# The expert layer of a fused conv, attention and mixture kernel: its two halves interleaved, pooling on column tiles, scatter by image pairs

## What is computed

```python
t = t + attn(ln(t)); t = t + ffn(ln(t))        # t: (16, 3136, 32); _L1_ffn_ref:
logits = einsum('bsd,ed->bse', x, gate_w) + gate_b          # 16 experts
probs = softmax(logits, axis=1)                              # over the positions
topv, topi = top_k(probs, 8)                                 # 8 positions per image and expert
pooled = einsum('bked,bke->bed', x[topi], topv)              # weighted sum of the 8 tokens
h = gelu([pooled, 1] @ weight1[e])                           # 33 -> 128
out = [h, 1] @ weight2[e]                                    # 129 -> 32
outputs[b, topi] += topv * out                               # scattered back
```

## Time and profile before

| | us |
|---|---|
| median of 3 runs (lowest, highest) | 3361.59 (3358.89, 3364.82) |
| the profiled execution's own time | 3363.74 |
| its span, first to last instruction | 3361.9 |
| mean granted TensorE clock, share of full | 0.951 |
| last attention instruction on PE ends | 3157.3 |
| first half of the expert layer starts on PE | 3169.96 |
| second half starts on PE | 3252.42 |
| last addition ends, stores start | 3334.5 |

### The profile page before, as it was taken

How to read it: one execution, slowest core, us unless ns; L and a number is a source line. 1 busy time by engine, 2 the same in 40 slices (tenths; PEclk the granted TensorE clock), 3 DMA queues, 4 the chain that set the end, 5 groups by cost and what they waited for, 6 DMA issues and landing times.

```text
span 3361.9 us, 66302 instructions
## 1 busy us (share of the span) xinstructions
PE 2950.1 (88%) x23401; PEld 1258.3 (37%) x23401; DVE 2471.9 (74%) x3210; ACT 2200.9 (65%) x3825; POOL 619.9 (18%) x497
## 2 busy tenths in 40 slices
PE   3788888888868999999999999999999999999775
PEld 2444444444435233333333333333333333333354
DVE  6788888888847877767777767777777777787342
ACT  2477776676755577767767767767777776777520
POOL 0444444444430101101101101001001011011100
PEclk7899999999989899999999999999999999999876
DMA  3000000000018010110110110101101101100022
GB/s 83 6 15 14 14 14 14 14 14 14 14 56 303 7 20 1 20 21 1 20 21 1 21 20 2 21 3 19 20 2 20 20 2 21 20 1 1 7 37 40
DMA packets 130451, 81.57 MB, mean 24 GB/s; under 512 B 111285, under 2 KB 120086, under 8 KB 129174
## 3 DMA queue, kind: packets, MB, share of 16 engines
q1 hardware_dynamic: 128629, 78.26, 9.5%
q10 hardware_dynamic: 1568, 0.04, 0.0%
HBM read 39.57 MB, written 32.11 MB: 21 GB/s over the span
## 4 chain that ended last, share of the span: by engine, by line
PE 59%; DVE 14%; issue 12%; POOL 6%; ACT 6%; DMA 2%; ACTq 1%; POOLq 0%; SPq 0%; DVEq 0%
PE ps L1531 18%; PE ps L1508 15%; PE ps L1478 14%; DVE arena L1117 7%; POOL arena L512 3%; PE ps L1541 2%; POOL arena L518 2%; ACT arena L667 1%; ACT L693 1%; PE ps L1358 1%; PE ps L1590 1%; PE ps L1490 1%; DMA arena<-in_x 1%; DVE arena L964 1%; POOL arena L528 1%
## 5 line engine op out<-in xcount | busy, mean ns | idle before, releaser
L1117 DVE TENSOR_REDUCE arena<-ps 128x2 f32<-128x896 f32 (+1 forms) x1408 | 1485.1, 1082 | 460.6 <-PE ps L1478 447.1
L800 ACT ACTIVATE arena<-ps 128x512 f32<-128x512 f32 (+1 forms) x2464 | 1377.4, 595 | 553.8 <-PE ps L1508 543.4
L1508 PE MATMUL ps<-arena 97*128 97x512 f16 (+1 forms) x2800 | 898.9, 360 | 24.6 <-issue 20.0
L1478 PE MATMUL ps<-arena 96*128 96x448 f16 x2800 | 775.9, 360 | 36.0 <-DVE arena L1117 27.1
L1531 PE MATMUL ps<-arena 128*32 128x512 f32 (+1 forms) x6176 | 685.4, 521 | 17.5 <-DVE arena L1139 17.0
L1508 PEld LDWEIGHTS ps<-arena 97*128 97x128 f16 (+1 forms) x2800 | 255.7, 100 | 708.0 <-ACT arena L800 462.5
L1478 PEld LDWEIGHTS ps<-arena 96*128 96x128 f16 x2800 | 256.8, 99 | 322.7 <-DVE arena L1117 108.3
L577 POOL TENSOR_TENSOR tok<-arena,tok 128x128 f32 (+3 forms) x112 | 47.9, 427 | 1585.4 <-DVE arena L1139 1585.4
L518 POOL TENSOR_TENSOR arena<-arena 113x784 f32<-113x784 f32 x128 | 192.4, 1503 | 428.9 <-DVE arena L967 428.9
L1531 PEld LDWEIGHTS ps<-arena 128*32 128x32 f32 x6176 | 131.5, 111 | 255.0 <-ACT arena L800 138.7
L512 POOL TENSOR_TENSOR arena<-arena 113x784 f32<-113x784 f32 x128 | 192.2, 1502 | 128.6 <-DVE arena L958 128.6
(11 more groups left out here) (180 smaller groups left out, 2787.5 us busy)
## 6 DMA issues: line engine op xcount, KB each, us to landing
arena<-qk_scratch SPq DMA_DIRECT2D x96, 196.0 KB, 4.1
qk_scratch<-arena SPq DMA_DIRECT2D x16, 448.0 KB, 4.9
arena<-ximg SPq DMA_DIRECT2D x16, 400.0 KB, 7.0
arena<-in_x SPq DMA_DIRECT2D x4, 1568.0 KB, 8.5
xa_scratch<-arena SPq DMA_DIRECT2D x32, 196.0 KB, 1.9
res_scratch<-arena SPq DMA_DIRECT2D x32, 196.0 KB, 2.1
arena<-xa_scratch SPq DMA_DIRECT2D x4, 1568.0 KB, 8.0
arena<-res_scratch SPq DMA_DIRECT2D x4, 1568.0 KB, 11.9
```

What stands on the lines that cost most here:

```text
L800: act.activation(pk[0:rows, x % DEPTH, QC * m:QC * m + n], ps[0:rows, w % SB, 0:n], ACT.Exp, scale=float(C) ** -0.5).then_inc(att["exp"], 1)
L1117: dve.tensor_reduce(mxp[0:rows, p, 2 * u:2 * u + k], ps[0:rows, at_:at_ + k, 0:KN], AX_X, ALU.max)\
L1478: last = pe.matmul(ps[0:rows, MB + 2 * (j % 2) + n % 2, 0:KN], q2[p][0:96, T * t:T * t + rows], k2[p][0:96, KN * m:KN * m + KN], start=Tru ...
L1508: last = pe.matmul(ps[0:rows, bank, at_ % QC:at_ % QC + chunk_cols(c)], k2[p][0:97, T * t:T * t + rows], q2[p][0:97, QC * c:QC * c + chunk ...
```

## The change

1. The halves are taken in the order `HALVES = (1, 0)`: first slots 8 to 15, which do not hold the last image. Only the second half's token columns wait for `att["xf"]`.
2. The last image's difference, square and product move from POOL to DVE, between its copies; the power stays on POOL.
3. Token columns and logits go chunk by chunk (up to 512 positions), with both groups of a chunk side by side: logits of a chunk are two matmuls, 64 output partitions each, and one ACT copy of all 128. In the first half ACT copies group 0 and DVE group 1, in the second ACT both. `token_exp(0)` stands on ACT ahead of chunk 1 of the second half, `token_scale(0)` ahead of chunk 5.
4. Selection: `not_equal` goes; ACT scales the exponentials by the reciprocal in two parts, DVE makes one product for each.
5. `mt` is copied by ACT alone. Pooling is one matmul for each image and tile (200 a half), 32 output partitions (a column tile) and 16 columns; 4 ACT copies take the result.
6. The bias of the second expert matrix is added by DVE in the copy to `eo` (`w2b` as 32 x 16), so the 16 one-row matmuls go.
7. Scatter goes by image pair: for each pair `r` and tile one matmul over 32 rows of `mk` with 64 columns, up to 8 tiles in a bank, and 4 DVE additions a pair. 200 matmuls a half.
8. PE's order interleaves the second half's pooling and experts with the first half's scatter.
9. Stores wait for one pair (4 additions) and issue its two images. The expert weights are loaded before attention's loop; ACT and DVE wait for the stores of `qk_scratch` before image 0, since buffers moved onto their source.

```diff
+        HALVES = (1, 0)
-            sp.wait_ge(att["xf"], B + 1)
-            for h in range(B // PB):
-                sp.wait_ge(moe["add"], NT * (h + 1))
+            for o in range(2):
+                for r in range(PB // 2):
+                    sp.wait_ge(moe["add"], 16 * o + 4 * r + 4)
...
+            act.wait_ge(prep["stored_a"], 64 * G)
+            act.wait_ge(prep["stored_b"], 64 * G)
...
@@ ACT @@
+            for n in range(NX):
+                token_columns(0, n, 0)
+                if n:
+                    logits_copy(0, n - 1)
+            logits_copy(0, NX - 1)
+            for n in range(NX):
+                if n == 1:
+                    token_exp(0)
+                if n == 5:
+                    token_scale(0)
+                token_columns(1, n, 0)
+                token_columns(1, n, 1)
+                if n:
+                    logits_copy(1, n - 1)
+            logits_copy(1, NX - 1)
+            weights_copy(0)
+            token_exp(1)
+            token_scale(1)
+            pooled_copy(0)
+            expert_gelu(0)
+            weights_copy(1)
+            pooled_copy(1)
+            expert_gelu(1)
...
@@ DVE @@
+            token_columns(0)
+            dve.memset(pooled[C:C + 1, :, :], 1.0).then_inc(moe["ones"], 1)
+            token_columns(1)
             sum_slot(B)
             mean_slot(B)
+            token_columns(2)
+            center_last()
+            token_columns(3)
+            square_last()
+            token_columns(4)
             square_sum(B)
             variance_slot(B)
+            token_columns(5)
+            token_columns(6)
+            normalize_last()
+            top_tokens(0)
+            top_tokens(1)
+            expert_out(0)
+            for r in range(4):
+                add_pair(0, r)
+            expert_out(1)
+            for r in range(4):
+                add_pair(1, r)
...
-                        last = pe.matmul(ps[:, 7, 64 * gg:64 * gg + 64], xf[0:rows, t, GB * g:GB * g + GB, :].rearrange("p b c -> p (b c)"),
-                                         mt[0:rows, t, 64 * gg:64 * gg + 64], start=(t == 0), stop=(t == NT - 1))
+                        for j in range(GB):
+                            b = GB * gg + j
+                            last = pe.matmul(ps[C * j:C * j + C, 7, E * gg:E * gg + E], xf[0:rows, t, half_slot(o, b), :],
+                                             mt[0:rows, t, E * b:E * b + E], start=(t == 0), stop=(t == NT - 1),
...
-                    pe.matmul(ps[0:rows, 3 + t % 4, 0:PB * C], mk[:, T * t:T * t + rows], bdo[:, :], start=True, stop=True)\
+                        last = pe.matmul(ps[0:rows, tg, 2 * C * (t % 8):2 * C * (t % 8 + 1)],
+                                         mk[o][C * r:C * r + C, T * t:T * t + rows],
+                                         bdo[C * r:C * r + C, :, :].rearrange("p b c -> p (b c)"), start=True, stop=True)
...
@@ PE @@
+            for o in range(2):
+                if o:
+                    pe.wait_ge(att["xf"], B + 1)
+                for n in range(NX):
+                    token_columns(o, n)
+                    if n:
+                        logits(o, n - 1)
+                logits(o, NX - 1)
+            weight_rows(0)
+            pool_tokens(0)
+            expert_hidden(0)
+            expert_out(0)
+            out_rows(0)
+            weight_rows(1)
+            scatter_pair(0, 0)
+            pool_tokens(1)
+            scatter_pair(0, 1)
+            expert_hidden(1)
+            scatter_pair(0, 2)
+            expert_out(1)
+            scatter_pair(0, 3)
+            out_rows(1)
+            for r in range(4):
+                scatter_pair(1, r)
```

More of the change, by code:

```diff
@@ L820, in _ @@
                         sums_copy(B - 1, c)
[L823 to L841, removed]
@@ new lines, in expert_gelu @@
+            def expert_gelu(o):
+                act.wait_ge(moe["hid"], o + 1)
+                if o:
+                    act.wait_ge(moe["out"], 1)
+                act.activation(eh[:, :], ps[:, 4, 0:E * PB], ACT.Gelu).then_inc(moe["gelu"], 1)
+            for n in range(NX):
[12 more added lines that the diff above has]
+                    logits_copy(1, n - 1)
@@ L1207, in _ @@
[L1207 to L1242, removed]
-                    dve.wait_ge(moe["scat"], NT * h + t + 1)
-                    v = tok[0:rows, PB * h:PB * (h + 1), t, :]
-                    dve.tensor_tensor(v, v, ps[0:rows, 3 + t % 4, 0:PB * C].rearrange("p (b c) -> p b c", b=PB), ALU.add)\
-                       .then_inc(moe["add"], 1)
@@ new lines, in token_columns, with logits @@
+                    last.then_inc(moe["xft"], 1)
+            def logits(o, n):
+                f = o * NX + n
+                for gg in range(2):
+                    pe.wait_ge(moe[f"xftc{gg}"], f + 1)
+                if f >= 3:
+                    pe.wait_ge(moe["logitc"], f - 2)
+                for gg in range(2):
+                    last = pe.matmul(ps[64 * gg:64 * gg + 64, f % 3, 0:chunk_cols(n)],
+                                     wgate[:, :, :].rearrange("p j e -> p (j e)"), xft[:, f % 3, gg, 0:chunk_cols(n)],
+                                     start=True, stop=True)
+                last.then_inc(moe["logit"], 1)
@@ new lines, in weight_rows @@
+            def weight_rows(o):
+                pe.wait_ge(moe["mk"], 2 * o + 2)
+                for n in range(NX):
+                    if o == 0 and n == 0:
+                        pe.wait_ge(moe["logitc"], 2 * NX)
+                    if NX * o + n >= 4:
+                        pe.wait_ge(moe["mtc"], NX * o + n - 3 if n >= 4 else NX * o)
+                    for t in chunk_tiles(n):
+                        rows = tile_rows(t)
+                        last = pe.transpose(ps[0:rows, n % 4, 128 * (t % 4):128 * (t % 4) + 128],
+                                            mk[o][:, T * t:T * t + rows], ident(128))
@@ L1669, in _, with expert_hidden @@
+                last.then_inc(moe["pool"], 1)
+            def expert_hidden(o):
+                pe.wait_ge(moe["poolc"], o + 1)
+                if o:
+                    pe.wait_ge(moe["gelu"], 1)
+                else:
+                    pe.wait_ge(moe["weights"], 48)
+                    pe.wait_ge(moe["ones"], 1)
                 for e in range(E):
-                    last = pe.matmul(ps[:, 0, PB * e:PB * (e + 1)], w1e[:, e, :], pooled[:, e, :], start=True, stop=True)
+                    last = pe.matmul(ps[:, 4, PB * e:PB * (e + 1)], w1e[:, e, :], pooled[:, e, :], start=True, stop=True)
@@ new lines, in scatter_pair @@
+            def scatter_pair(o, r):
+                if r == 0:
+                    pe.wait_ge(moe["bdo"], o + 1)
+                for tg in range(4):
+                    if o or r:
+                        pe.wait_ge(moe["add"], 16 * o + 4 * r + tg - 3)
+                    elif tg == 0:
+                        pe.wait_ge(moe["mtc"], 2 * NX)
+                    for t in range(8 * tg, min(8 * tg + 8, NT)):
+                        rows = tile_rows(t)
+                        last = pe.matmul(ps[0:rows, tg, 2 * C * (t % 8):2 * C * (t % 8 + 1)],
+                                         mk[o][C * r:C * r + C, T * t:T * t + rows],
+                                         bdo[C * r:C * r + C, :, :].rearrange("p b c -> p (b c)"), start=True, stop=True)
+                    last.then_inc(moe["scat"], 1)
```

232 lines of the change are left out of this document (154 added, 78 removed).

## The result

The changed kernel takes 3336.7 us (median of 4 runs, 3336.0 to 3343.74) against 3362.61 of the kernel before on the same chip (3358.89 to 3364.82): ratio 0.9929, 95% interval 0.9912 to 0.9946. It is faster by 25.9 us, less than half of the 57.6 forecast. The profiled execution took 3336.39 us, its span is 3334.2, the mean granted clock 0.946.

What follows compares the result with a forecast made beforehand. The prediction took the end after attention to be a chain of engines waiting for each other, not one busy engine. Its path summed to a span of 3304.6 us, 57.3 less, giving 3304 us at the median, range 3284 to 3352.

Steps and rivals of the forecast that it cites:

- weight rows, first half: Seven ACT copies behind the first half's weight-row transposes, 4.7 us, to 3198.7.
- to the pooled copy: First half's pooling, 5.0 us on PE, hidden under ACT's 6.2 us until free; four copies then end at 3206.0.
- experts, first half: First product 5.6 us, gelu and handovers 0.6, second product 3.3, addition and transpose 0.7; to 3216.2.
- the clock's 1.1: Second half's transposes at 0.21 us each, counted as 1.1 us of clock loss.
- PE's last stretch: Eight scatter pairs at 5.9 us, 47.2, plus second half's pooling, experts and 2.2 us of waits: 63.3 us, to 3284.4.
- the forecast's own signs of a wrong sum: Sum wrong if a scatter pair takes 11.8 us, pooling outlasts ACT's scalings, or the attention loop's period changes.
- First half's tokens, last image's norm: After attention, the first half's token work overlaps the norm; DVE's product ends at 3172.9, with that half's logits done.
- Second half's tokens: PE stalls about 4 us, then ACT is the bound for 17.4 us, to 3194.0.
- Stores: Issues take 3.2 us an image; second half's begin at 3267.6 and land at 3294.9, about 10 us after the last addition.
- Clock: Scatter runs 4.3 us at 0.50 before rising, losing 2.15 us ahead of four pairs: 8.6 us; second half's transposes 1.1.
- its first rival: Half clock through all scatter: scatter 47.2 us more, second pooling 5 more, total 3346 us; chance 0.20.
- pooling: 400 instructions a half at 0.0125 us, 5.0 us; the first half's lies under the 6.2 us until ACT is free.

Runs made afterwards that it cites:

- norm_first: Changed kernel with the last image's norm done alone, ahead of both halves' token columns; 3350.83 us, ratio 0.9965.
- two_row_groups: Changed kernel with two scatter pairs taken at once, on two groups of 32 rows and into different banks; 3303.52 us, ratio 0.9832.
- the fours: Changed kernel with scatter by four images, 128 columns a matmul: quads128 3296.23 us, quads64 3302.44 us.
- rows128: Changed kernel with each scatter pair's matmuls over all 128 rows, other pairs' rows of bdo zero; 3338.44 us, ratio 0.9928.
- warm128: rows128 with four extra matmuls of 512 columns ahead of the second half's scatter; 3327.96 us, ratio 0.9902.
- quads64: quads128 with each scatter matmul over only the 64 rows of its four images; 3302.44 us, ratio 0.9827.
- old_pooling: Changed kernel with the earlier pooling matmuls, 50 of 128-wide weights and 64 columns a half instead of 200 on column tiles; 3349.5 us, ratio 0.9958.
- quads128: Changed kernel with scatter by four images, 128 columns, over all 128 rows with other rows of bdo zero; 3296.23 us, ratio 0.9802.
- spread_pooling: two_row_groups with the second half's pooling matmuls placed between the first double's scatter matmuls; 3312.0 us, ratio 0.9847, result not the reference's.

## Why the prediction was partly right

Each step from attention's end, forecast against measured in the changed kernel:

| step | forecast | measured | difference |
|---|---|---|---|
| to the second half's tokens | 15.6 | 15.6 | 0.0 |
| tokens and logits of the second half | 21.1 | 22.1 | +1.0 |
| weight rows, first half | 4.7 | 5.5 | +0.8 |
| to the pooled copy | 7.3 | 10.6 | +3.3 |
| experts, first half | 10.2 | 9.6 | -0.6 |
| second weight rows, with the clock's 1.1 | 6.0 | 6.3 | +0.3 |
| PE's last stretch, with the clock's 8.6 | 71.9 | 105.3 | +33.4 |
| to the span's end | 10.5 | 8.5 | -2.0 |
| tail | 147.3 | 183.6 (the rows add to 183.5) | +36.3 |

Less the 6.5 us by which attention's last instruction came earlier, and 0.2 because the forecast counts from that instruction's end (3157.3) and the measured column from its start, this is the 29.6 us between the forecast span, 3304.6, and 3334.2. A change of the attention loop was one of the forecast's own signs of a wrong sum. It came, 10.7 us between the two profiles. Since attention also began 4.2 us later, 6.5 us of it reach the total, and without them the miss would be larger.

*Right:* "First half's tokens, last image's norm" and "Second half's tokens", the second to 1 us; by norm_first the overlap is worth 11.0 us. "Stores": issues of 3.2 us an image, without pause behind PE only where scatter is faster than they are (two_row_groups, the fours), and 8 us instead of 27 behind the last addition here.

*The step that failed* is "Clock". It took from the earlier trace rows that scatter comes back to 1.00 after 4.3 us, and charged 2.15 us for each of four recoveries. The row was L1685's, 128 rows and 256 columns. The pairs have neither. In their place the runs showed: 32-row pairs begun at 1.00 fell to 0.50 in every kernel that had them, and did not come back in 84.7 us of work; the same pairs over 128 rows did not come back either in 43.3 us, but kept 1.00 in two of the three places where they began at it (5.7 us in rows128, 23 us in warm128, against the fall after 2.5 us in warm128's first pair). So "PE's last stretch" went at 0.217 us an instruction and not at 0.118: 84.5 us for the eight pairs against 55.8 with the forecast's clock losses, 28.7 of the 36.3. The forecast had this as its first rival, at 0.20 and 3346. Scatter came out 9.9 us below the rival's 94.4, because half clock costs 10.84 us a pair and not 11.8, and the first pair still had part of its time at 1.00 (8.67); the total, 3336.7, also owes 6.5 us to attention, against which stand the longer steps of the table. The rows did not change a pair's price at one clock: at 0.50 a pair of 32 rows took 10.89 us and one of 128 rows 10.91. The Trainium skill says so on the page that the forecast names (TensorE: Matmul & The Clock Gate), but in the section Why this matters for your kernels and not in Part 3; that other row groups run side by side is shown by two_row_groups.

*Mis-sized:* pooling. The pace was right, 4.94 us of work for 400 instructions against 5.0: 128 of them in 1.50 us are 11.7 ns each, so the forecast did well to go by its row and not by the floor of about 25 ns in the Trainium skill (TensorE: Matmul & The Clock Gate, section Back-to-back issue gap), which does not hold for this row. Missing were the stops: 4.4 us in the first half, which outlast the scalings that should have hidden pooling (+3.3), and 5.0 in the second, which with 5.8 us of work, part of it at 0.50, make 10.8 instead of 5.0 (+5.8). Against that the second expert product took 1.9 us and not 3.3, while the first took 6.8 and not 5.6.

So the overlap works as forecast, and the gain was lost mainly to slower work on the path, 400 scatter instructions in 84.5 us (350 of them wholly at half clock), where before 50 of 128 rows and 256 columns took 13.6 us a half. A smaller part went with pooling, 3.3 us in the first half and 5.8 in the second.

*Open:* why the first pair of warm128 lost the clock that the same pair of rows128 kept; what the chip goes by when it grants or takes the clock, of which the runs show only outcomes for single shapes, mostly from one profile each; and why attention's loop was shorter in every profile of a changed kernel.

## What to carry to other kernels

A matmul's price taken from a row holds at that row's clock: before a matmul is cut into smaller ones, look in the trace for a stretch of the new shape that began at half clock, not one that kept full clock; if there is none, price it at half clock too. Splitting work for an earlier start of stores is worth it in the largest pieces that still start them early: fours of 128 columns over all rows cost at 1.00 what pairs of 64 did, instruction for instruction. Where small matmuls can't be made larger, two row groups at once are worth trying: here they halved the time even at half clock.

## What the runs showed that was not expected

- PE busy without a gap and at half clock: 43.3 of 43.3 us (rows128), 32.5 of 32.5 (quads64), 22.0 of 22.0 (old_pooling). The Trainium skill (TensorE: Matmul & The Clock Gate, section Part 1: The HAM clock gate) ties the clock to how active the engine has been; by these rows a stretch that the profile calls fully busy can stay at 0.50.
- Zeros in 64 more rows were faster than leaving the rows out: quads128 against quads64, 11.8 against 22.3 us for the same 100 instructions.
- 400 pooling instructions stopped after 145 and again after 128 more, for 2.15 and 2.24 us. Each of those 128 has a weight load beside it, so 256 instructions lie between stops, and the DMA view of the changed kernel shows what ran at that time (columns: packets, MB, share of 16 engines, from 3193.9 to 3204):

```profile
q8 instruction: 3, 0.05, 2.0%
```

  In the second pooling, with stores beside it, the stops were 1.7 and 3.3 us. They keep to a count of instructions, not to a place: with 50 scatter instructions ahead, as in the changed kernel, the second pooling first stops after 243, with 100 ahead, as in two_row_groups, after 193. From the last stop of the first pooling this makes 510 instructions on PE in both, near four times 128.

```profile
3228.22 2.89 PE L1794 MATMUL ps<-arena,ximg 128*32 128x16 f32 x193
3232.81 1.38 PE L1794 MATMUL ps<-arena,ximg 64*32 64x16 f32 x128 [1.70 <-issue]
```

  The Trainium skill (Runtime: NRT & Kernel Launch, section Instruction fetch mechanics) has instructions fetched in blocks of 256, at a cost that is mostly hidden. The number agrees; hidden it was not, where a block lasts 1.5 us. That old_pooling had no stops, and spread_pooling none in its second half's pooling, fits this; that the fetch is what PE waited for is argued, not shown.
